# Attention block on one core: the layer-1 probabilities change partition quarters by way of memory in place of sixteen direct moves

## The chip, the cores and the metric

The kernel runs on one core of a Trainium2 chip. TensorE (PE; its weight loads are shown as PEld) multiplies, VectorE (DVE), ScalarE (ACT) and GpSimd (POOL) work on tiles in the on-chip memory SBUF, which has 128 partitions, and SyncE (SP) issues nearly all DMAs, which 16 DMA engines carry out. Each engine runs its own instructions in order, and the engines meet at semaphores. The metric is the time of one execution on the device in microseconds (us), as a median of several runs.

## What is computed

Two layers follow each other on an input of 8 batches, 512 channels and 32x32 = 1024 tokens. Layer 0 is a group norm, an attention with 8 heads, a projection and a second group norm with a residual. Layer 1, cut to what matters here, is an attention over all 512 channels:

```python
qkv = einsum('oc,bcn->bon', w_qkv, x)             # x: 8 x 512 x 1024 tokens
qkv = qkv / (sqrt(mean(square(qkv), axis=1)) + 0.0001)
q, k, v = split(qkv, 3, axis=1)
attn = softmax(einsum('bci,bcj->bij', q, k) * 512 ** -0.5, axis=-1)
h = einsum('bij,bcj->bci', attn, v)               # sums over j
out = (x + einsum('oc,bcn->bon', w_out, h)) * 2.0 ** -0.5
```

For each batch `attn` is a matrix of 1024x1024 float32 probabilities. The scores leave TensorE with the query token i on the partitions. The product with v sums over the key token j, so the probabilities have to be turned until j lies on the partitions. The change is in this turning.

## The kernel before, in words

The eight batches run one after the other: a hardware loop of seven and a last one written out, with the same body. In a batch come layer 0 (64 steps of scores, softmax, transposes and products, the longest part), its projection and second norm, and then layer 1, which is the stretch that matters here:

- **Scores.** TensorE computes eight blocks `scores1(0)` to `scores1(7)`, each of 128 query tokens by 1024 keys (48 matmuls at L514). VectorE scales a block and takes its row maxima (`scaled_max`, L1493), ScalarE takes the exponential (`exps1`, L1047), VectorE the reciprocal of the row sum (`recip1`, L1499), and GpSimd multiplies the block by it (`normalise`, L1097). Normalised block i lies in `PB[:, i, :]`, 128 partitions by 1024 columns. ScalarE writes the columns so that the four quarters of 256 columns of a block are what has to go to the four quarters of 32 partitions (`by_quarter`).
- **Exchange.** The blocks are handled in two halves, c = 0 (blocks 0 to 3) and c = 1 (blocks 4 to 7). When the last block of a half is normalised, SyncE moves the half from PB into `F`, which is the 128x4096 weight tile `W[0]`: partition quarter tq of the source, column quarter sq, goes to partition quarter sq of F. These are 16 DMAs a half (L484), each from 32 partitions to 32 partitions, 128 runs of 1 KB. Their 16 increments each go to `s_exchanged`.
- **Turning.** VectorE waits for all 16 moves and then transposes 32x32 squares out of F back into PB, one call `turn(c, s)` (L1522) for each of eight key blocks s. ScalarE copies the turned block as the high part of a split into two parts of lower precision (`turned_hi`, L1057), and VectorE subtracts it for the low part (`turned_lo`, L1528).
- **Products.** TensorE multiplies with v (`values1(c, e, s)`, L819): for a half first e = 0 and 1 together, six matmuls for each s, which waits for the low part of that s, then e = 2 and 3. A half is 96 matmuls.

The order on each engine is written out by hand. On VectorE: `scaled_max(6)`, `turn(0,0)` to `turn(0,3)` with `recip1(6)` between them, `turned_lo(0,0)` and `(0,1)`, `scaled_max(7)`, the other turns and low parts of half 0, the norm of the next batch's input, `layer_out(0)` to `(2)` (L1505), then `turn(1,0)`, `turn(1,1)`, `turned_lo(1,0)` and so on. The last normalise of half 1 comes on GpSimd after `scaled_max(7)`. On SyncE the exchange of half 0 stands behind a weight load (L475), that of half 1 behind that of half 0 and behind a wait for all eight turns of half 0 (`s_e_ready`, since F is used again), and behind both stand the stores of the output (L495) and a weight load into `W[0]` (L491) that waits for the last turn of half 1.

Of the kernel before, what the change touches and what calls it, by code (L numbers as in the profile page):

```python
# [16 lines left out]
B, C, N = 8, 512, 1024  # L17
HEADS = 8
CH = C // HEADS
P = 128  # L20
KB = C // P
# [10 lines left out]
f32 = mybir.dt.float32  # L32
# [46 lines left out]
LAG = 5  # L79
CREDIT = 1  # L80
QUARTERS = 4
EXCHANGE = QUARTERS * QUARTERS * 16


def build(nc, x, wv_t, wp_t, wqk_t, v_qkv, v_out, wo_t, vecs, consts, out):
    ctx = ExitStack()
    with ctx:
        def sb(name, shape, dt=f32):
            return ctx.enter_context(nc.sbuf_tensor(name, shape, dt))
# [4 lines left out]
        def sem(name):  # L94
            return ctx.enter_context(nc.semaphore(name))
# [6 lines left out]
        d_m = nc.dram_tensor("d_m", [P, 4096], f32)  # L102
        d_u = nc.dram_tensor("d_u", [P, 4096], f32)
        d_r = nc.dram_tensor("d_r", [N], f32)

        X = sb("X", [P, KB, N])
        XA = sb("XA", [P, KB, N])
# [4 lines left out]
        PB = sb("PB", [P, 8, N])  # L112
# [45 lines left out]
        F = W[0][:, :].bitcast(f32).rearrange("p (q t n) -> p q t n", q=QUARTERS, t=KB)  # L158

        def turned(c, s):  # L160

            return PB[:, 4 * c + s // 2, HALF * (s % 2):HALF * (s % 2) + HALF]
# [28 lines left out]
        def w_qk(pair):  # L191

            w = W[1 if pair < 2 else 0][:, 2048 * (pair % 2):2048 * (pair % 2) + 2048]
            return w.rearrange("p (h k n) -> p h k n", h=2, k=KB)
# [55 lines left out]
        s_p_norm = sem("p_norm")  # L250
# [23 lines left out]
        s_prod_sum = sem("prod_sum")  # L274
        s_sum_full = sem("sum_full")
        s_g_full = sem("g_full")
        s_exchanged = sem("exchanged")
        s_e_ready = sem("e_ready")
        s_slot_read = sem("slot_read")
# [67 lines left out]
        def big_count(b, key):  # L347

            return BIG_BASE + b * NBIG + big_at(b, key) + 1
# [5 lines left out]
        def own_wait(eng):  # L355

            eng.sem_inc(s_waited, 1)

        def src_x(b):
            return x[b].rearrange("(k p) n -> p k n", p=P)  # L360
# [3 lines left out]
        def _(sp):  # L364
# [39 lines left out]
            def stack_head(b, pair, head):  # L404

                rows = slice(64 * head, 64 * head + 64)
                s_stack = (s_stack_a, s_stack_b)[head]
                sp.wait_ge(s_nat_ready, b * 16 + 4 * pair + 4)
                own_wait(sp)
                if pair:  # L410
                    sp.wait_ge(s_big_full, big_count(b, ("s", 16 * (pair - 1) + 8 * head + 7)))
                    own_wait(sp)
                elif head:
                    sp.wait_ge(s_stack_a, (b * PAIRS + 1) * 96)
                    own_wait(sp)
                moves = [("q", 64 * head, 0, 0), ("q", 64 - 64 * head, 0, 1)]
                moves += [("kh", q, 1, 0) for q in (0, 64)] + [("kl", q, 1, 1) for q in (0, 64)]
                for kind, to, what, part in moves[::1 if pair or head else 2]:
                    sp.dma_start(stack(kind, head)[to:to + 64, :].bitcast(f32),  # L419
                                 unstacked(what, part)[rows, :].bitcast(f32))\  # L420
                      .then_inc(s_stack, 16)

            def body(b, last):

                sp.wait_ge(s_o_full, b * 24 + CREDIT)
                own_wait(sp)
                sp.wait_ge(s_stored_g, 16)
                sp.wait_ge(s_stored_m, 16)
                stack_head(b, 0, 0)
                sp.wait_ge(s_stored_qk, 48)  # L430
                own_wait(sp)
                sp.dma_start(w_qk(1).rearrange("p h k n -> p (h k n)").bitcast(f32), d_qk[1]).then_inc(ld_qk[1], 16)
                stack_head(b, 0, 1)

                sp.wait_ge(s_out_done, (b * 8 + CREDIT) * 16)
                own_wait(sp)
                sp.dma_start(X[:], src_x(b)).then_inc(s_x_res, 16)
                sp.wait_ge(s_v_full, b * 4 + 4)
                own_wait(sp)
                for i in (2, 3):  # L440
                    sp.dma_start(w_qk(i).rearrange("p h k n -> p (h k n)").bitcast(f32), d_qk[i]).then_inc(ld_qk[i], 16)
                stack_head(b, 1, 0)
                sp.dma_start(W[1][:].bitcast(f32), d_wp[:]).then_inc(s_ld_wp, 16)
                stack_head(b, 1, 1)
                stack_head(b, 2, 0)
                stack_head(b, 2, 1)
                stack_head(b, 3, 0)
                sp.wait_ge(s_stored_wv, 16)
                own_wait(sp)
                sp.dma_start(W[0][:].bitcast(f32), d_g[:]).then_inc(s_ld_g, 16)  # L450
                stack_head(b, 3, 1)
                sp.wait_ge(s_big_full, big_count(b, ("proj", KB - 1)))
                own_wait(sp)
                sp.dma_start(W[1][:].bitcast(f32), d_m[:]).then_inc(s_ld_m, 16)
                if not last:
                    sp.wait_ge(s_xc_ready, (b + 1) * KB)
                    sp.wait_ge(s_xc_lo, (b + 1) * KB)
                    own_wait(sp)
                    sp.dma_start(XA[:], src_x(b + 1)).then_inc(s_x_next, 16)
                sp.wait_ge(s_g_full, b * 2 + 2)  # L460
                own_wait(sp)
                sp.wait_ge(s_stored_u, 16)
                own_wait(sp)
                sp.dma_start(W[0][:].bitcast(f32), d_u[:]).then_inc(s_ld_u, 16)
                sp.wait_ge(s_r_col, b + 1)
                own_wait(sp)
                sp.dma_start(d_r.ap().rearrange("(s p) -> p s", p=P), rcol, allow_slow_non_contiguous=True)\
                  .then_inc(s_r_stored, 16)
                sp.wait_ge(s_r_stored, b * 16 + 16)
                own_wait(sp)  # L470
                sp.dma_start(RB[:], d_r.ap().partition_broadcast(P)).then_inc(s_r_row, 16)
                if not last:
                    sp.wait_ge(s_big_full, big_count(b, ("y", KB - 1)))
                    own_wait(sp)
                    sp.dma_start(w_qk(0).rearrange("p h k n -> p (h k n)").bitcast(f32), d_qk[0])\  # L475
                      .then_inc(ld_qk[0], 16)
                for c in range(2):
                    sp.wait_ge(s_p_norm, b * 72 + 64 + 4 * c + 4)
                    if c:
                        sp.wait_ge(s_e_ready, b * 16 + 8)  # L480
                    own_wait(sp)
                    for tq in range(QUARTERS):
                        for sq in range(QUARTERS):
                            sp.dma_start(F[32 * sq:32 * sq + 32, tq, :, :],  # L484
                                         PB[32 * tq:32 * tq + 32, 4 * c:4 * c + 4, 256 * sq:256 * sq + 256])\
                              .then_inc(s_exchanged, 16)
                for j in range(8):
                    if j == 3 and not last:
                        sp.wait_ge(s_e_ready, b * 16 + 16)
                        own_wait(sp)  # L490
                        sp.dma_start(W[0][:].bitcast(f32), d_wv[:]).then_inc(s_ld_wv, 16)  # L491
                    sp.wait_ge(s_y_out, b * 8 + j + 1 + CREDIT)
                    own_wait(sp)
                    c, e = j // 4, j % 4
                    sp.dma_start(out[b].rearrange("(k p) n -> p k n", p=P)[:, e, HALF * c:HALF * c + HALF],  # L495
                                 X[:, e, HALF * c:HALF * c + HALF]).then_inc(s_out_done, 16)

            sp.dma_start(d_wv[:], W[0][:].bitcast(f32)).then_inc(s_stored_wv, 16)
            sp.wait_ge(s_prod_lo, SETUP_BIG)
            sp.dma_start(d_u[:], product_stage(2).bitcast(f32)).then_inc(s_stored_u, 16)  # L500
            each_batch(sp, body)
            sp.wait_ge(s_out_done, (B * 8 + CREDIT) * 16)

# [668 lines left out]
        def _(dve):  # L1172
# [130 lines left out]
            def body(b, last_batch):  # L1303
# [215 lines left out]
                def turn(c, s):  # L1519
                    if s == 0:  # L1520
                        dve.wait_ge(s_exchanged, (2 * b + c + 1) * EXCHANGE)
                    V.transpose(turned(c, s).rearrange("p (t q r) -> p t q r", t=KB, q=QUARTERS),  # L1522
# [110 lines left out]
```

## Time and profile before

| | us |
|---|---|
| median of 3 runs | 3375.08 (3374.36 to 3375.76) |
| the profiled execution | 3375.88 |
| its span, first to last instruction | 3373.7 |
| TensorE busy in the span | 3351.2 (99%) |
| VectorE busy | 2132.7 (63%) |
| ScalarE busy | 1838.7 (55%) |
| GpSimd busy | 1064.3 (32%) |

All durations below come from the one profiled execution. A row of a timeline gives the start in us from the span's start, the length in us, engine, line, operation, the tiles as written <- read, and a count where neighbours are merged; in square brackets stand the engine's idle time just before and who ended it. L numbers are lines of the kernel. A row of a table by stretches gives, for each engine, the busy time and the number of instructions, then the granted TensorE clock (1.00 is the full 2.4 GHz), the mean busy share of the 16 DMA engines and what they moved. In the names of tiles, F shows as W, of which it is a view.

### The profile page before, as it was taken

To read this page: it belongs to the slowest core of one execution; us is meant where nothing else is said; L and a number is where in the kernel's file an instruction comes from. 1 tells how busy PE (TensorE), PEld (TensorE's weight loads), DVE (VectorE), ACT (ScalarE), POOL (GpSimd) and SP (SyncE) were. 2 spreads that over 40 slices of the span, in tenths; PEclk is the share of its full clock that TensorE was granted. 3 is DMA by queue.
4 is the path that set the end of the run, shared out by engine and by line. 5 is a ranking of instruction groups with operands and counts; after the bars stand their busy time and mean duration, and the time that the engine had idled before them with its cause. 6 is when DMAs were issued, how large, how long until landed. Compare 5 with 4: busy or idle time off the path is not lost.

```text
span 3373.7 us, 51950 instructions
## 1 busy us (share of the span) xinstructions
PE 3351.2 (99%) x16816; PEld 2777.5 (82%) x16816; DVE 2132.7 (63%) x3489; ACT 1838.7 (55%) x3094; POOL 1064.3 (32%) x947
## 2 busy tenths in 40 slices
PE   8999999999999999999999999999999999999999
PEld 6888888888888888888888888888888888888887
DVE  5677357773578745786457854578555784557844
ACT  4677227862378523784337842388333882347822
POOL 1344104441045410453104531145211452124511
PEclk9999999999999999999999999999999999999999
DMA  8522244313534125331253212442224422343212
GB/s 340 149 67 59 79 131 124 93 34 94 140 99 101 62 57 151 103 86 76 53 167 91 73 75 76 144 101 63 93 61 144 98 63 94 92 139 70 63 57 75
DMA packets 109871, 332.15 MB, mean 98 GB/s; under 512 B 21760, under 2 KB 54784, under 8 KB 98816
## 3 DMA queue, kind: packets, MB, share of 16 engines
q1 hardware_dynamic: 107648, 322.15, 33.3%
q10 hardware_dynamic: 1920, 6.29, 0.9%
q8 instruction: 149, 2.44, 0.3%
q14 instruction: 154, 1.26, 0.1%
HBM read 162.68 MB, written 31.49 MB: 58 GB/s over the span
## 4 chain that ended last, share of the span: by engine, by line
PE 94%; DMA 2%; issue 1%; DVE 1%; SPq 1%; ACT 1%; POOL 0%; POOLq 0%; DVEq 0%
PE big L514 25%; PE big L648 14%; PE ops L634 14%; PE tps L619 14%; PE big L746 7%; PE big L655 5%; PE tps L819 5%; PE ops L819 5%; PE ops L598 3%; DMA ST<-ST 2%; PE tps L746 1%; SPq L419 0%; PE ops L746 0%; SPq L484 0%; PE ops L788 0%
## 5 line engine op out<-in xcount | busy, mean ns | idle before, releaser
L1097 POOL TENSOR_SCALAR PB<-PB,small 128x1024 f32<-128x1024 f32 x576 | 648.7, 1127 | 1294.8 <-DVE small L1342 1277.2
L1347 DVE TENSOR_TENSOR PT<-tps,PT 128x512 fp32r<-128x512 f32 x1024 | 652.5, 679 | 42.1 <-ACT PT L954 41.7
L1336 DVE TENSOR_REDUCE small<-big 128x1 f32<-128x1024 f32 x512 | 625.2, 1221 | 85.1 <-PE big L648 81.8
L954 ACT ACTIVATE PT<-tps 128x512 fp32r<-128x512 f32 x1024 | 564.1, 597 | 158.3 <-PE tps L619 155.4
L948 ACT ACTIVATE PB<-big,small 128x1024 f32<-128x1024 f32 x512 | 572.8, 1119 | 94.8 <-DVE small L1336 91.8
L634 PE MATMUL ops<-PT,VT 128*128 128x512 f32 x2048 | 599.1, 414 | 0.0
L648 PE MATMUL big<-ST 128*128 128x512 f32 x2048 | 554.2, 392 | 3.5 <-DMA ST<-ST 3.5
L619 PEld LDWEIGHTS tps<-ident,PB 128*128 128x128 f32 x4096 | 470.2, 140 | 95.4 <-DVE PT L1347 30.9
L619 PE MATMUL tps<-ident,PB 128*128 128x128 f32 x4096 | 545.7, 274 | 0.9
L648 PEld LDWEIGHTS big<-ST 128*128 128x128 f32 x2048 | 382.6, 188 | 91.5 <-issue 6.1
L634 PEld LDWEIGHTS ops<-PT,VT 128*128 128x128 f32 x2048 | 346.1, 189 | 47.1 <-DVE PT L1347 5.0
L514 PE MATMUL big<-HH,W 128*128 128x512 f32 x1024 | 333.9, 391 | 0.8 <-issue 0.7
L1328 DVE SCALAR_TENSOR_TENSOR ST<-big,vec,ST 128x512 fp32r<-128x512 f32 x128 | 96.1, 751 | 318.8 <-ACT ST L940 318.8
L940 ACT ACTIVATE ST<-big,vec 128x512 fp32r<-128x512 f32 x128 | 88.2, 689 | 293.4 <-PE big L514 293.4
L514 PEld LDWEIGHTS big<-HH,W 128*128 128x128 f32 x1024 | 192.3, 188 | 44.7 <-issue 3.7
L1107 POOL TENSOR_TENSOR XA<-RB 64x512 f32<-64x512 f32 x128 | 163.9, 1280 | 146.9 <-ACT RB L965 145.7
L1047 ACT ACTIVATE PB<-PB,small 128x1024 f32<-128x1024 f32 x56 | 69.8, 1246 | 252.1 <-POOL small L1160 252.1
L514 PE MATMUL big<-HL,W 128*128 128x512 f32 x512 | 199.9, 390 | 0.0
L1160 POOL TENSOR_SCALAR small<-small 128x1 f32<-128x1 f32 x64 | 19.0, 297 | 518.8 <-DVE small L1493 505.4
L514 PE MATMUL big<-HH,ST 128*128 128x512 f32 x512 | 178.5, 389 | 0.0
L655 PE MATMUL big<-HH,W 128*128 128x512 f32 x512 | 168.6, 393 | 0.0
L1493 DVE CUSTOM_DVE_ANT_0 PB<-big,RB 128x1024 f32<-128x1024 f32 x56 | 68.6, 1225 | 151.4 <-PE big L514 151.4
(188 smaller groups left out, 4911.7 us busy)
## 6 DMA issues: line engine op xcount, KB each, us to landing
ST<-ST SPq DMA_DIRECT2D x360, 256.0 KB, 5.3
W<-d_qk SPq DMA_DIRECT2D x32, 1024.0 KB, 7.0
W<-PB SPq DMA_DIRECT2D x256, 128.0 KB, 2.4
X<-in_x SPq DMA_DIRECT2D x8, 2048.0 KB, 10.2
W<-d_wp SPq DMA_DIRECT2D x8, 2048.0 KB, 11.9
W<-d_g SPq DMA_DIRECT2D x8, 2048.0 KB, 11.8
W<-d_m SPq DMA_DIRECT2D x8, 2048.0 KB, 7.7
W<-d_u SPq DMA_DIRECT2D x8, 2048.0 KB, 13.2
```

The source lines that it names most:

```text
L514: last = mm(dst, stat(sp_, k), mov(mp_, k), start=(i == 0), stop=(i == n - 1))
L619: last = nc.tensor.transpose(tps[n % 2][:, P * t:P * t + P], PB[:, 4 * (u % 2) + t, P * s:P * s + P], ident[:])
L634: last = mm(ops[u % 2][:], VT[:, s, P * (u // 2):P * (u // 2) + P], pt_slot(u, s)[:, part, :], start=(s == 0 and part == 0), stop=(s == 7 ...
L648: last = mm(t[:, cols], stack("q", head)[:, tok:tok + P], stack(kind, head)[:, cols], start=(i == 0), stop=(i == 1))
L655: last = mm(t[:, cols], w_full[1][:, wp, k, P * o:P * o + P], (HH, HL)[ap][:, k, cols], start=(k == 0 and i == 0), stop=(k == PAIRS - 1 an ...
L746: last = mm(to, w_full[slot][:, wp, j, P * k:P * k + P], x1(xp, j)[:, cols], start=(j == 0 and i == 0), stop=(j == (k if slot == 0 else KB ...
L819: last = mm(out_bank(use)[:], VT[:, s, col:col + P], ptb[:, pp, :], start=(s == 0 and i == 0), stop=(s == 7 and i == 2))
L948: act_fn(PB[:, i, :], t[:], ACT.Exp, bias=negmax[:, i:i + 1], accum_out=rowsum[:, i:i + 1])\
L954: act_fn(pt_slot(u, s)[:, 0, :], tps[n % 2][:], ACT.Copy).then_inc(s_pt_hi, 1)
L1097: nc.gpsimd.tensor_scalar(PB[:, i, :], PB[:, i, :], rinv[:, i:i + 1], 1.0, ALU.mult, ALU.mult)\
L1336: V.tensor_reduce(negmax[:, i:i + 1], tile(("s", 4 * u + tb))[:], axis=AX.X, op=ALU.max, negate=True).then_inc(s_row_max, 1)
L1347: V.tensor_tensor(pt_slot(u, s)[:, 1, :], tps[n % 2][:], pt_slot(u, s)[:, 0, :].bitcast(f32), ALU.subtract).then_inc(s_pt_ready, 1)
```

## The change

Each half now goes through a buffer `d_f[c]` in the memory off the core. As soon as a block is normalised, SyncE stores it whole, 128 partitions by 4 KB, 512 KB in one DMA; the buffer's layout puts partition p of quarter q at `[p, q, t, :]`. After the fourth store SyncE waits for all four to have landed (`s_sent`), for half 1 also for the turns of half 0 as before, and then loads F with four DMAs, one for each partition quarter: 32 partitions, each of 16 runs of 1 KB, 512 KB in one DMA. VectorE now waits for the four loads. The transposes and all that comes after are the same. The diff, whole:

```diff
-EXCHANGE = QUARTERS * QUARTERS * 16
+EXCHANGE = QUARTERS * 16
...
+        d_f = [nc.dram_tensor(f"d_f{c}", [P // QUARTERS, QUARTERS, KB, N], f32) for c in range(2)]
...
+        s_sent = sem("sent")
...
                 for c in range(2):
-                    sp.wait_ge(s_p_norm, b * 72 + 64 + 4 * c + 4)
+                    for t in range(KB):
+                        sp.wait_ge(s_p_norm, b * 72 + 64 + 4 * c + t + 1)
+                        own_wait(sp)
+                        sp.dma_start(d_f[c].ap().rearrange("p q t n -> q p t n")[:, :, t, :], PB[:, 4 * c + t, :])\
+                          .then_inc(s_sent, 16)
+                    sp.wait_ge(s_sent, (2 * b + c + 1) * 16 * KB)
                     if c:
                         sp.wait_ge(s_e_ready, b * 16 + 8)
                     own_wait(sp)
-                    for tq in range(QUARTERS):
-                        for sq in range(QUARTERS):
-                            sp.dma_start(F[32 * sq:32 * sq + 32, tq, :, :],
-                                         PB[32 * tq:32 * tq + 32, 4 * c:4 * c + 4, 256 * sq:256 * sq + 256])\
-                              .then_inc(s_exchanged, 16)
+                    for q in range(QUARTERS):
+                        sp.dma_start(F[32 * q:32 * q + 32, :, :, :], d_f[c][:, :, :, 256 * q:256 * q + 256])\
+                          .then_inc(s_exchanged, 16)
```

## Rows read from the trace of the kernel before

**Rows 1.** The page: span, busy time of TensorE, granted clock in 40 slices.

```profile
span 3373.7 us, 51950 instructions
PE 3351.2 (99%) x16816; PEld 2777.5 (82%) x16816; DVE 2132.7 (63%) x3489; ACT 1838.7 (55%) x3094; POOL 1064.3 (32%) x947
PEclk9999999999999999999999999999999999999999
```

**Rows 2.** Waits over the whole span: who for whom, us in total, times, longest.

```profile
DVE PB L1522 <- DMA W<-PB: 15.9, 9, 2.4
PEld ops L819 <- DVE ST L1528: 3.7, 8, 0.5
PEld ops L819 <- DVE PT L1528: 1.7, 5, 0.4
```

**Rows 3.** Timeline of SyncE's queue in the sixth batch, both exchanges and behind.

```profile
2483.85 34.90 SPq L484 DMA_DIRECT2D W<-PB  x32
2519.01 1.72 SPq L495 DMA_DIRECT2D out<-X  x3
```

**Rows 4.** Timeline of GpSimd, sixth batch: normalise of blocks 3, 4 and 7.

```profile
2482.63 1.13 POOL L1097 TENSOR_SCALAR PB<-PB,small 128x1024 f32<-128x1024 f32 x1 [0.66 <-DVE small L1499]
...
2491.65 1.13 POOL L1097 TENSOR_SCALAR PB<-PB,small 128x1024 f32<-128x1024 f32 x1
...
2506.51 1.13 POOL L1097 TENSOR_SCALAR PB<-PB,small 128x1024 f32<-128x1024 f32 x1 [0.81 <-DVE small L1499]
```

**Rows 5.** Timeline of VectorE, sixth batch: first turns, first low parts, scaled_max(7).

```profile
2496.82 1.90 DVE L1522 STREAM_TRANSPOSE PB<-W 128x512 f32<-128x512 f32 x3
...
2499.52 1.27 DVE L1528 TENSOR_TENSOR PT<-PB,PT 128x512 fp32r<-128x512 f32 x2
2501.62 1.23 DVE L1493 CUSTOM_DVE_ANT_0 RB<-big,RB 128x1024 f32<-128x1024 f32 x1 [0.83 <-PE big L514]
...
2520.58 1.30 DVE L1522 STREAM_TRANSPOSE PB<-W 128x512 f32<-128x512 f32 x2 [1.75 <-DMA W<-PB]
2522.07 0.69 DVE L1528 TENSOR_TENSOR PT<-PB,PT 128x512 fp32r<-128x512 f32 x1 [0.19 <-ACT PT L1057]
```

**Rows 6.** Timeline of TensorE's weight loads, sixth batch: where the products begin.

```profile
2501.01 5.40 PEld L819 LDWEIGHTS ops<-PT,VT 128*128 128x128 f32 x24
...
2508.23 1.23 PEld L819 LDWEIGHTS ops<-ST,VT 128*128 128x128 f32 x6 [0.46 <-DVE ST L1528]
...
2523.10 5.40 PEld L819 LDWEIGHTS ops<-PT,VT 128*128 128x128 f32 x24
```

**Rows 7.** Timelines, half 1 of batches 2 and 5: last normalise, first turn.

```profile
853.00 1.13 POOL L1097 TENSOR_SCALAR PB<-PB,small 128x1024 f32<-128x1024 f32 x1 [0.81 <-DVE small L1499]
866.44 1.30 DVE L1522 STREAM_TRANSPOSE PB<-W 128x512 f32<-128x512 f32 x2 [1.11 <-DMA W<-PB]
...
2092.85 1.13 POOL L1097 TENSOR_SCALAR PB<-PB,small 128x1024 f32<-128x1024 f32 x1 [0.81 <-DVE small L1499]
2107.63 1.30 DVE L1522 STREAM_TRANSPOSE PB<-W 128x512 f32<-128x512 f32 x2 [2.43 <-DMA W<-PB]
```

**Rows 8.** The page's DMA issues: count, KB of each, median us from issue to landing.

```profile
out<-X SPq DMA_DIRECT2D x64, 256.0 KB, 2.4
RB<-d_r SPq DMA_DIRECT2D x8, 512.0 KB, 5.1
d_u<-PT SPq DMA_DIRECT2D x1, 2048.0 KB, 9.6
W<-d_m SPq DMA_DIRECT2D x8, 2048.0 KB, 7.7
```

**Rows 9.** Three stretches: moves ST<-ST, the exchange W<-PB, the load W<-d_m.

```profile
2152.00:2154.00 2.00, 2.00 (x10) 1.50 (x8) 0.00 (x0) 0.00 (x0) 0.00 (x0) 1.00 1.00 207
...
2488.00:2490.00 2.00, 2.00 (x11) 1.71 (x10) 0.02 (x1) 0.00 (x0) 0.00 (x0) 1.00 0.87 198
...
3227.00:3229.00 2.00, 2.00 (x12) 1.68 (x11) 1.64 (x6) 0.00 (x0) 0.01 (x1) 1.00 1.03 442
```

## The prediction

> **What bounds the kernel now.** I read the page first. TensorE is busy 99% of the span at the full granted clock [rows 1], so nothing can be won but the few waits left in its stream, and whatever makes it wait longer is added to the time. The list of waits comes next: at the products of layer 1 TensorE's weight loads wait for low parts of turned blocks, 3.7 us in eight waits and 1.7 us in five [rows 2]. VectorE waits 15.9 us in nine waits for the exchange itself [rows 2]. So the exchange sits right at the edge of TensorE's work, and the question is how much later, or earlier, F may be full.
>
> The timelines of the sixth batch answer that. I measure an exchange from the end of the last normalise of its half to the first turn and call that length E. In half 0 the normalise ends at 2482.63 + 1.13 = 2483.76 [rows 4], the first of the 16 moves is issued at 2483.85 [rows 3] and the first turn starts at 2496.82 [rows 5]: 13.06 us, with no wait in front of it. The first low part is done at about 2500.15, half of the pair that starts at 2499.52 [rows 5], and TensorE takes it at 2501.01 without a wait [rows 6], so there is 0.86 us to spare. Behind that low part stands scaled_max(7), which waits 0.83 us for TensorE [rows 5], the same slack. **Half 0 may take 13.06 + 0.85 = 13.9 us** before TensorE stands, and from there every microsecond moves both TensorE and VectorE, and by scaled_max(7) also the last normalise of half 1.
>
> In half 1 the normalise ends at 2507.64 [rows 4], and the first turn starts at 2520.58 after 1.75 us of waiting for the moves [rows 5]: E = 12.9. The first low part ends at 2522.76 [rows 5] and TensorE takes it at 2523.10 [rows 6]: **half 1 may take 12.94 + 0.34 = 13.3 us.** The eight batches vary; the shortest and the longest E of half 1 are 866.44 - 854.13 = 12.3 and 2107.63 - 2093.98 = 13.65 [rows 7]. The long ones are the waits of TensorE for PT, 1.7 us in all [rows 2], about 0.2 us a batch.
>
> **The change, part by part.**
>
> Removed: 32 issues a batch on SyncE and their moves. They ran at about 198 GB/s with the DMA engines busy at 0.87 [rows 9]; a half of 2048 KB (2097 thousand bytes) takes 10.6 us at that, and the rest of E is the way from issue to landing. SyncE's own time costs nothing: only the stores of the output stand behind it [rows 3], and no engine of this batch waits for them.
>
> Stores of the first three blocks of a half: each is issued while later blocks are still computed. The fourth normalise of a half is the last thing before the exchange, so these three are landed or nearly so by then and cost nothing; block 2 of half 0 is finished only 1.8 us before block 3, and if its 512 KB were still moving this would cost up to a part of its own length.
>
> The fourth store is new on the path. Two stores in the trace bracket it: 256 KB lands after 2.4 us, 2048 KB after 9.6 us [rows 8]. On the line between them 512 KB is 3.4 us. The bounds are 2.4 us and, by the 512 KB load, 5.1 us [rows 8]. I take 3.4.
>
> The wait on s_sent and the issue of the loads: the gap between the end of the normalise and the first issue is 0.09 us today [rows 3, 4]; I take 0.1 us twice, once for the store and once for the loads. Queued behind the waiting SyncE are the loads themselves, for half 0 the stores of half 1, and for half 1 the output stores.
>
> The loads move the same 2048 KB into F. No row shows a load from memory into 32 partitions. The nearest row by size and source is W<-d_m, the same 2048 KB into all 128 partitions: 7.7 us to landing [rows 8], at 442 GB/s in its middle [rows 9], so 4.7 us of it is transfer and 3.0 us is start and end. The nearest rows by destination are the moves between parts of the partitions: ST<-ST, 64 partitions at a time with runs of 4 KB, holds the engines at a share of 1.00 and yet moves 207 GB/s, and the exchange of today, 32 at a time with runs of 1 KB, 198 GB/s [rows 9]. So long runs do not help a move that touches half of the partitions or fewer, and I take 207 GB/s for the loads, since each one writes 32 partitions and they follow each other in one queue: 10.1 us of transfer plus 3.0 is **13.1 us**. Bounds: 7.7 us if the loads run as W<-d_m does, 13.6 us at 198 GB/s.
>
> The Trainium skill, page "SBUF — State Buffer", section "Door 1: The DMA port swizzle", states that what a transfer can reach depends on how many of 16 ports its partitions touch, and that 32 or 64 partitions from 0 touch 8, for HBM to SBUF 189 GB/s at 1 MiB with about 218 GB/s as the limit. No row here shows such a load; at 218 GB/s the transfer would be 9.6 us and the sum below 3416 us.
>
> Sum: E = 0.1 + 3.4 + 0.1 + 13.1 = **16.7 us** in place of about 13. Half 0: 16.7 - 13.9 = 2.8 us of TensorE. Half 1, counted from a last normalise that is late by the same 2.8 us as TensorE is: 16.7 - 13.3 = 3.4 us, less the 0.2 us that it waits there now, 3.2. Together 6.0 us a batch. Eight batches: 48 us. The stall of 0.46 us inside half 0 [rows 6] stays, since VectorE and TensorE shift together. Nothing later gives the time back: TensorE is the engine that is behind, and the others wait for it. The profiled execution took 3375.88 us, 0.8 us above the median of the three runs and 2.2 us more than its span; 3375.9 + 48 = **3424 us**.
>
> The granted clock is at its full level in every slice [rows 1], the first included. I price the longer stands of TensorE at no loss of clock; no row shows a stand of 3 us in mid-kernel.
>
> **The rivals.**
>
> *The loads run at full width* (the other side: not slower). If what holds ST<-ST and W<-PB is their source, which is also a part of the partitions, a load from memory is free of it. Then it takes 7.7 us, E = 0.2 + 3.4 + 7.7 = 11.3, half 0 has no wait it has not now, half 1 loses its 0.2 us: 8 x 0.2 = 1.5 us won, 3374 us. For it: both slow rows have a narrow source as well as a narrow target, so they can't tell which of the two binds. Against it: each load writes 32 partitions only, and today's 16 moves go round all four target quarters and are no quicker for it. It decides from E = 14.1 on, where (14.1 - 13.9) + (14.1 - 13.3) - 0.2 is 0.8 us a batch, 0.2% in all; that is a load of 10.5 us, or 280 GB/s.
>
> The Trainium skill, page "DMA: Bandwidth & Descriptors", section "Anatomy of one DMA — SWDGE (gpsimd) path", gives about 2.0 us plus bytes/436e3 for a DMA, and its "Rules for kernel authors" advise to make few large transfers of many small. By that the loads together would take 6.8 us and a store of 512 KB 3.2 us, and the time would come out as in this rival. The trace agrees for W<-d_m, 7.7 us, and not for ST<-ST at 207 GB/s [rows 8, 9].
>
> *Between the two*: the quarters overlap in part, and the loads run at 230 to 280 GB/s. Then a load takes 10.5 to 12.1 us, E = 14.1 to 15.7, and the time is 3383 to 3408 us.
>
> *The stores of half 1 cross the loads of half 0.* Block 4 is normalised at 2492.78 [rows 4], in the middle of loads that would run from 2487 to 2500, and its 512 KB store goes to the same engines. In today's kernel nothing is moved then but the exchange. If the store takes its share ahead of the loads' tail, half 0 is 512 KB at 207 to 442 GB/s later, 1.2 to 2.5 us, 10 to 20 us in all: 3434 to 3444 us. Against it: it is issued after the loads in the same queue.
>
> *A dearer store.* At 5.1 us [rows 8] E is 18.4, and the time is 8 x (4.5 + 4.9) = 75 us more, 3451 us.
>
> **How the numbers follow.** Forecast, E between 15.7 and 17.5, 3408 to 3437 us: 0.55. Crossing stores: 0.13. Between: 0.12. Full width: 0.16. Dearer store: 0.04. The range from 3385 to 3445 leaves out the full width and the dearest store, some 0.2. Faster by over 0.2% (6.75 us, about what a measurement of this kernel can tell from no change) is hardly possible: the exchange stands for no more than 1.7 us of TensorE's waits [rows 2]; I give it 0.02. Within 0.2%: the full width and the quickest end of what lies between, 0.15. Slower: 0.83.
>
> **What would show it.** The wait of VectorE for the exchange at L1522 should grow from 15.9 us in nine waits to some 70 in sixteen, 3.6 us in half 0 and about 5.5 in half 1, and TensorE should wait at L819 for PT 5 to 6 us a batch where it waits 0.2. The issue list should show stores at 3 to 4 us and loads at 11 to 13 us, and the stretch of the loads some 210 GB/s at a share near 1. The wait of 0.46 us for ST should stay. A rate above 280 GB/s in that stretch would make the prediction wrong, and so would a first turn of half 0 that still starts within 13.9 us of the normalise.

## The result, and the profile after

| | before | after |
|---|---|---|
| median | 3375.64 us (6 runs) | 3581.72 us (6 runs) |
| ratio | | 1.061, 95% interval 1.0596 to 1.0623 |
| span of the profiled execution | 3373.7 us | 3579.6 us |

The changed kernel is 206 us slower, 25.8 us a batch. The direction was forecast, the size was not: the forecast was 48 us more, and its range ended at 3445 us.

The page of the changed kernel, as in [rows 1]: span, busy times, and the granted TensorE clock in 40 slices.

```profile
span 3579.6 us, 51942 instructions
PE 3386.7 (95%) x16816; PEld 2801.5 (78%) x16816; DVE 2133.0 (60%) x3489; ACT 1841.6 (51%) x3094; POOL 1066.5 (30%) x947
PEclk9999999999999999999999998999989999899998
```

TensorE runs the same 16816 matmuls, and yet it is busy 3386.7 us in place of 3351.2, 35.5 us more, and the clock is no longer full in every slice. The list of waits, as in [rows 2], has the rest:

```profile
DVE PB L1527 <- DMA W<-d_f: 199.3, 16, 13.4
PE ops L824 <- DVE PT L1533: 170.6, 16, 12.1
```

And the waits of SyncE's queue:

```profile
SPq L359 <- DMA d_f<-PB: 199.0, 16, 12.8
```

TensorE now stands 170.6 us before the first product of the 16 halves. With the 35.5 us of slower matmuls that is 206.1 us, the whole difference of the spans (205.9). And SyncE waits 199.0 us, 12.4 us in the mean of the halves, for the stores to land, which the forecast had put at 3.4 us.

The timelines of the sixth batch, as in [rows 3 to 6]: SyncE's stores and loads (the second row is the fourth store of half 0 alone, from a narrower window), then the normalise of block 3 on GpSimd, the first turn on VectorE and the first products on TensorE.

```profile
2600.38 13.19 SPq L483 DMA_DIRECT2D d_f<-PB  x4
...
2613.06 0.51 SPq L483 DMA_DIRECT2D d_f<-PB  x1
2626.51 2.62 SPq L490 DMA_DIRECT2D W<-d_f  x4
2629.32 19.33 SPq L483 DMA_DIRECT2D d_f<-PB  x4
2660.96 2.59 SPq L490 DMA_DIRECT2D W<-d_f  x4
...
2611.83 1.13 POOL L1102 TENSOR_SCALAR PB<-PB,small 128x1024 f32<-128x1024 f32 x1 [0.67 <-DVE small L1504]
...
2638.31 1.90 DVE L1527 STREAM_TRANSPOSE PB<-W 128x512 f32<-128x512 f32 x3 [12.21 <-DMA W<-d_f]
...
2641.56 7.42 PE L824 MATMUL ops<-PT,VT 128*128 128x512 f32 x24 [10.97 <-DVE PT L1533]
```

In half 0, E is 2638.31 - 2612.96 = 25.35 us, where 16.7 was forecast. From the issue of the fourth store to the issue of the loads pass 13.45 us, from there to the first turn 11.8 us. The 24 matmuls behind the wait take 7.42 us; in the kernel before, the same row of TensorE's timeline has 5.60:

```profile
2501.24 5.60 PE L819 MATMUL ops<-PT,VT 128*128 128x512 f32 x24
```

Four stretches of the changed kernel show what the DMA engines and the clock did, with the columns of [rows 9]: the stores, then the loads, then the end of the wait.

```profile
2614.00:2618.00 4.00, 4.00 (x19) 3.30 (x19) 1.14 (x3) 1.33 (x2) 0.27 (x1) 1.00 0.26 97
...
2632.00:2634.00 2.00, 0.00 (x0) 0.00 (x0) 0.00 (x0) 0.00 (x0) 0.00 (x0) 1.00 1.13 223
2634.00:2636.00 2.00, 0.00 (x0) 0.00 (x0) 0.00 (x0) 0.00 (x0) 0.00 (x0) 0.74 1.13 216
2636.00:2640.00 4.00, 0.00 (x0) 0.00 (x0) 1.69 (x3) 0.94 (x2) 0.00 (x0) 0.50 0.53 134
```

The share in the stores is a quarter, 0.26, at 97 GB/s: as if four of the sixteen engines carried them. The loads ran close to the 207 GB/s that were forecast, at 216 to 223 GB/s with all engines busy. And the granted clock falls to 0.50, the level of 1.2 GHz, while TensorE stands.

A second row of the page speaks for four engines, that of the DMA packets, here of the kernel before and then of the changed one:

```profile
DMA packets 109871, 332.15 MB, mean 98 GB/s; under 512 B 21760, under 2 KB 54784, under 8 KB 98816
```

```profile
DMA packets 115247, 365.69 MB, mean 102 GB/s; under 512 B 18944, under 2 KB 51968, under 8 KB 104192
```

If each DMA leaves one small packet for each engine that it runs on, and moves and loads run on all sixteen, the 256 direct moves left 4096 of the 21760 and the 64 loads leave 1024. Then 18944 - (21760 - 4096) - 1024 = 256 are left for the 64 stores: four each.

The theory from here on: **a DMA runs on as many engines as its outermost dimension allows, and the store, whose target is ordered by quarter, partition, column, has 4 outermost.** Rivals: going through memory is dear in itself; the layout of the buffer, with 64 KB from one partition's row to the next, is what slows the stores; the fourth store is only late because it stands behind the third.

### The profile page after: what moved, and what is told of

It is laid out like the page before. It is cut to its first block, busy times and chain, and to the rows that moved or that the text cites. A ratio compares the mean times of both kernels' runs of the same rounds, so it can differ in the third digit from the quotient of the medians.

```text
span 3579.6 us, 51942 instructions
## 1 busy us (share of the span) xinstructions
PE 3386.7 (95%) x16816; PEld 2801.5 (78%) x16816; DVE 2133.0 (60%) x3489; ACT 1841.6 (51%) x3094; POOL 1066.5 (30%) x947
## 2 busy tenths in 40 slices
DMA packets 115247, 365.69 MB, mean 102 GB/s; under 512 B 18944, under 2 KB 51968, under 8 KB 104192
## 4 chain that ended last, share of the span: by engine, by line
PE 80%; DMA 12%; issue 2%; DVE 2%; ACT 1%; SPq 1%; POOL 1%; POOLq 0%; DVEq 0%; ACTq 0%
PE big L519 20%; PE big L653 13%; PE ops L639 13%; PE tps L624 13%; PE big L751 6%; DMA d_f<-PB 6%; PE big L660 5%; DMA W<-d_f 5%; PE ops L824 3%; PE ops L603 2%; PE tps L824 2%; DMA ST<-ST 2%; PE tps L751 1%; SPq L490 1%; ACT PB L1052 1%
## 5 line engine op out<-in xcount | busy, mean ns | idle before, releaser
L639 PE MATMUL ops<-PT,VT 128*128 128x512 f32 x2048 | 599.2, 414 | 0.0
L639 PEld LDWEIGHTS ops<-PT,VT 128*128 128x128 f32 x2048 | 346.1, 189 | 47.3 <-DVE PT L1352 5.0
L519 PE MATMUL big<-HH,W 128*128 128x512 f32 x1024 | 333.9, 391 | 0.4
L824 PE MATMUL ops<-PT,VT 128*128 128x512 f32 x384 | 124.3, 495 | 170.6 <-DVE PT L1533 170.6
L824 PEld LDWEIGHTS ops<-PT,VT 128*128 128x128 f32 x384 | 94.7, 252 | 200.2 <-DVE PT L1533 154.9
L1527 DVE STREAM_TRANSPOSE PB<-W 128x512 f32<-128x512 f32 x128 | 86.1, 693 | 199.3 <-DMA W<-d_f 199.3
## 6 DMA issues: line engine op xcount, KB each, us to landing
W<-d_wp SPq DMA_DIRECT2D x8, 2048.0 KB, 12.3
```

The source lines that it names most:

```text
L519: last = mm(dst, stat(sp_, k), mov(mp_, k), start=(i == 0), stop=(i == n - 1))
L639: last = mm(ops[u % 2][:], VT[:, s, P * (u // 2):P * (u // 2) + P], pt_slot(u, s)[:, part, :], start=(s == 0 and part == 0), stop=(s == 7 ...
L824: last = mm(out_bank(use)[:], VT[:, s, col:col + P], ptb[:, pp, :], start=(s == 0 and i == 0), stop=(s == 7 and i == 2))
```

## Experiments

The edits are shown against the changed kernel, or against the run that is named, without their waits, semaphore increments and counts, and with `nc.dram_tensor` and `.ap()` shortened.

**One store with 128 rows outermost.** The buffer is ordered by partition; to keep the access patterns of the loads short, they become sixteen of 128 KB.

```diff
-d_f = [dram([P // QUARTERS, QUARTERS, KB, N]) for c in range(2)]
+d_f = [dram([P, KB, N]) for c in range(2)]
...
-sp.dma_start(d_f[c].rearrange("p q t n -> q p t n")[:, :, t, :], PB[:, 4 * c + t, :])
+sp.dma_start(d_f[c][:, t, :], PB[:, 4 * c + t, :])
...
-for q in range(QUARTERS):
-    sp.dma_start(F[32 * q:32 * q + 32, :, :, :], d_f[c][:, :, :, 256 * q:256 * q + 256])
+for tq in range(QUARTERS):
+    for q in range(QUARTERS):
+        sp.dma_start(F[32 * q:32 * q + 32, tq, :, :], d_f[c][32 * tq:32 * tq + 32, :, 256 * q:256 * q + 256])
```

> The buffer is laid out by partition, so that one store of a block has 128 rows outermost in memory as well as in PB; the loads become sixteen of 128 KB as the direct moves were. In the changed kernel a half took 25.4 us from its last normalise to the first turn, 13.4 of it until the fourth store had landed, and the DMA engines stood at a share of 0.25 all through the stores. Theory A, the stores run on 4 of the 16 engines because the buffer's outermost dimension is 4: now a store lands after some 3.4 us, the share in the stores is well above 0.25, the length is about 16 us, TensorE waits some 5 us a batch and the time is 3400 to 3420 us. Theory B, writing to memory and reading it back is dear in itself: the fourth store still takes over 10 us and the time stays above 3540 us.

Measured: 3413.73 us, ratio 1.0115 (1.0098 to 1.0132). Its DMA issues (columns of [rows 8]), then SyncE's wait for the stores, then the page's packets:

```profile
d_f<-PB SPq DMA_DIRECT2D x64, 512.0 KB, 2.6
W<-d_f SPq DMA_DIRECT2D x256, 128.0 KB, 3.0
```

```profile
SPq L359 <- DMA d_f<-PB: 38.1, 16, 2.8
```

```profile
DMA packets 119087, 365.71 MB, mean 107 GB/s; under 512 B 22784, under 2 KB 55808, under 8 KB 108032
```

The same 512 KB now land in 2.6 us. The wait for the stores falls from 199.0 to 38.1 us, and 168 of the 206 us are gone. The small packets are 17664 + 320 x 16 = 22784, sixteen for each of the 64 stores and 256 loads. E is 15.3 to 16.7 us in the halves of this run, where 16.7 was forecast. That memory is dear in itself falls.

**The buffer as it was, each store cut into four.**

```diff
-sp.dma_start(d_f[c].rearrange("p q t n -> q p t n")[:, :, t, :], PB[:, 4 * c + t, :])
+for q in range(QUARTERS):
+    sp.dma_start(d_f[c][:, q, t, :], PB[32 * q:32 * q + 32, 4 * c + t, :])
```

> The buffer's layout and the four loads stay as in the changed kernel; only the store of a block is cut into four, one for each partition quarter, so that 32 is outermost in each. Theory A (too few engines): the fourth block's stores land after 4 to 5 us, the length is about 16 to 17 us, the time 3405 to 3425 us. Theory C, the layout of the buffer (rows of one partition 64 KB apart) is what slows the stores: the stores stay at some 100 GB/s, the length stays at 25 us and the time above 3540 us, while the run with the other layout is quick.

Measured: 3434.71 us, ratio 1.0175 (1.0158 to 1.0192), 10 us above the expected range. Its DMA issues, and from the timeline of TensorE the first products of both halves in the sixth batch:

```profile
d_f<-PB SPq DMA_DIRECT2D x256, 128.0 KB, 2.3
W<-d_f SPq DMA_DIRECT2D x64, 512.0 KB, 7.9
```

```profile
2541.09 5.73 PE L824 MATMUL ops<-PT,VT 128*128 128x512 f32 x24 [1.17 <-DVE PT L1533]
...
2567.08 7.37 PE L824 MATMUL ops<-PT,VT 128*128 128x512 f32 x24 [3.68 <-DVE PT L1533]
```

With 32 outermost the stores into the same layout are quick, so the layout falls. E is 15.5 to 17.9 us. The 10 us above the range fit the clock: after a wait of 1.17 us the 24 matmuls take 5.73 us, after one of 3.68 us they take 7.37. The forecast's sum with this run's mean E, 16.0 and 17.1 us in the two halves, gives 46 of the 59 us by which its span is longer, and 13 us are left.

**Two outermost in place of four.** This asks the theory for a second size of the effect.

```diff
-sp.dma_start(d_f[c].rearrange("p q t n -> q p t n")[:, :, t, :], PB[:, 4 * c + t, :])
+for h in range(2):
+    sp.dma_start(d_f[c].rearrange("p q t n -> q p t n")[2 * h:2 * h + 2, :, t, :], PB[64 * h:64 * h + 64, 4 * c + t, :])
```

> The changed kernel with each store of a block cut into two of 256 KB, each with 2 outermost in memory where the whole store has 4. Theory, the outermost dimension sets how many of the 16 engines a store runs on: now two, a share of 0.13 and some 50 GB/s in the stores, which fall behind the blocks; a half takes over 40 us in the first half and over 30 in the second, and the time is 3700 us or more, although the stores are more in number. Rival, it is the size of one DMA or its runs of 4 KB: two stores at a time are no slower than one, and the time is at most 3580 us.

Measured: 3853.66 us, ratio 1.1416 (1.1394 to 1.1437). A stretch of its stores and one of its loads, then its packets:

```profile
2790.00:2794.00 4.00, 4.00 (x21) 3.40 (x20) 1.04 (x5) 0.89 (x2) 0.62 (x1) 1.00 0.13 53
...
2814.00:2818.00 4.00, 0.00 (x0) 0.00 (x0) 0.00 (x0) 0.00 (x0) 0.00 (x0) 0.50 1.03 219
```

```profile
DMA packets 115247, 365.69 MB, mean 95 GB/s; under 512 B 18944, under 2 KB 51968, under 8 KB 104192
```

Half the share, 0.13, and half the rate, 53 GB/s, although twice as many stores are under way: with four engines as with two, each carries some 24 to 27 GB/s. The 18944 small packets are those of the changed kernel, now for 128 stores in place of 64, so two each. At any time two engines carry the stores; whether both stores of a block share the same two, or one follows the other, no row shows, since none names the engines. E is 43 to 44 us in half 0 and about 42 in half 1, and both, like the time, are in what was expected (over 40, over 30, 3700 us or more).

The Trainium skill, page "DMA: Bandwidth & Descriptors", section "Why a DMA increments its semaphore by 16 and not by 1", states this rule: a DMA is split over the largest number of engines up to 16 that divides the slowest dimension of both sides, and a DMA that SyncE issues takes the lowest-numbered ones. The runs here agree with the number: 128 and 32 outermost run wide, 4 at a share of 0.26, 2 at 0.13. Which engines they are no run here shows.

**The fourth store without a third in front of it.** Only the stores of the first three blocks are cut.

```diff
+if t < KB - 1:
+    for q in range(QUARTERS):
+        sp.dma_start(d_f[c][:, q, t, :], PB[32 * q:32 * q + 32, 4 * c + t, :])
+else:
     sp.dma_start(d_f[c].rearrange("p q t n -> q p t n")[:, :, t, :], PB[:, 4 * c + t, :])
```

> The changed kernel, with the stores of the first three blocks of a half cut into quarters as in the run with quarter stores, and the fourth store left as it is, one DMA with 4 outermost. It parts the fourth store's own time from its wait behind the third. Theory: alone it moves 512 KB at 100 GB/s, 5.2 us, and lands after about 7 us; a half takes 19 us from the last normalise to the first turn, TensorE waits some 11 us a batch, and the time is 3455 to 3480 us with what the clock costs. Rival, the 13.4 us are all the fourth store's own: the half stays at 25 us and the time above 3560 us.

Measured: 3532.75 us, ratio 1.0467 (1.0447 to 1.0486), between the two. SyncE's timeline in the sixth batch, half 0, and two stretches of that store:

```profile
2583.84 0.61 SPq L487 DMA_DIRECT2D d_f<-PB  x1
2593.97 2.61 SPq L494 DMA_DIRECT2D W<-d_f  x4
```

```profile
2587.00:2590.00 3.00, 3.00 (x16) 2.50 (x15) 0.27 (x2) 0.53 (x2) 0.00 (x0) 1.00 0.24 51
2590.00:2593.00 3.00, 3.00 (x15) 2.47 (x14) 1.13 (x2) 1.33 (x2) 1.36 (x2) 1.00 0.18 75
```

Alone the fourth store still takes 10.1 us. By this run 10.1 of the 13.45 us of the changed kernel are its own, and 3.3 are the wait behind the third. The expected 7 us supposed the 97 to 103 GB/s of the busy queue; alone the four engines move 51 GB/s at a share of 0.24 first, and then 75 GB/s at a share of only 0.18. So they are slow in the store's first part and not in its last; why is not settled.

**What the clock costs.** TensorE is kept busy while it waits, with matmuls whose result the product overwrites.

```diff
 for c in range(2):
+    if c:
+        pe.wait_ge(s_y_out, b * 8 + 1 + CREDIT)
+    for i in range(48):
+        mm(ops[0][:], VT[:, 0, 0:P], x1(0, 0)[:, 0:HALF], start=True, stop=True)
     for s in range(NT):
         values1(c, 0, s)
```

> The changed kernel with 48 matmuls more of 512 columns before the first product of each half, into a bank that the product starts anew; they take 10.9 us of the 11 us in which TensorE waits. Theory of the clock: the granted clock stays at 1.00, the first 24 matmuls of each half take some 5.6 us where they took 7.4, and the time falls by 16 x 1.8 = 29 us to about 3553 us. Rival: these matmuls are slow because the low parts come one by one; then the time stays at 3582 us within 5.

Measured: 3565.23 us, 16.5 us less than the changed kernel, against 29 expected. The loads of the sixth batch's half 0 with the clock beside them, and the first products:

```profile
2617.00:2621.00 4.00, 4.00 (x20) 3.30 (x19) 0.00 (x0) 0.00 (x0) 0.00 (x0) 1.00 1.11 211
2621.00:2625.00 4.00, 4.00 (x19) 3.34 (x18) 0.00 (x0) 0.00 (x0) 0.00 (x0) 1.00 1.13 212
```

```profile
2631.02 5.74 PE L825 MATMUL ops<-PT,VT 128*128 128x512 f32 x24 [1.97 <-DVE PT L1538]
```

The clock stays at 1.00, but for one short stretch in the seventh batch, and the 24 matmuls take 5.74 us. So the slow matmuls are the clock's. Not all of the 35.5 us comes back, for two reasons. In three batches of this run E of half 0 is 27.2 to 27.3 us where the others have 25.4 to 26.0; why is open. And most of the rest was never lost. In the changed kernel the 96 products of half 0 take 14.4 us more than before, in all batches, and those of half 1 17.2. What half 0 loses is hidden: the last normalise of half 1 waits for VectorE and not for these products, so TensorE stands that much less at half 1, 79.0 us where the forecast's sum with the measured E has 93.6.

**The loads: narrow target or source in memory?** The stores do the permuting, to a buffer of [4, 32, 4, KB, 256], the layout of F, and F is loaded with one DMA of 128 partitions.

```diff
+to = d_f[c].rearrange("q p s t r -> p q s t r")
 for t in range(KB):
+    for tq in range(QUARTERS):
+        sp.dma_start(to[:, :, tq, t, :], PB[32 * tq:32 * tq + 32, 4 * c + t, :].rearrange("p (q r) -> p q r", q=QUARTERS))
...
+sp.dma_start(F.rearrange("p q t n -> p (q t n)"), d_f[c].rearrange("q p s t r -> (q p) (s t r)"))
```

> The stores do the permuting: each block goes out in four DMAs of 32 partitions, in runs of 1 KB, to a buffer that has the layout of F, and F is loaded whole with one DMA of 128 partitions after all four blocks have landed. Theory, a load into 32 partitions is held to some 210 GB/s by its narrow target: now the load takes about 7.7 us as the load of the weights does, the half 12 to 13 us, TensorE's waits are those of the kernel before and the time is 3372 to 3380 us. Rival, it is the source in memory that holds the loads: the load stays at 11 to 12 us, the half at 16 us and the time at 3410 us or more.

Measured: 3380.51 us, ratio 1.0017 (1.0008 to 1.0027). Its DMA issues and a stretch of the load:

```profile
W<-d_f SPq DMA_DIRECT2D x16, 2048.0 KB, 8.5
```

```profile
2494.00:2495.00 1.00, 1.00 (x6) 0.81 (x6) 0.07 (x2) 0.43 (x1) 0.73 (x2) 1.00 1.01 426
```

The same 2048 KB from memory now move at 426 GB/s, twice the rate of the loads into 32 partitions at the same share of the engines, and land after 8.5 us. The source in memory is not what held them. (The runs on the side of F are longer here, 16 KB, so width and length change together; the next run parts them.) E is 12.2 to 14.9 us in half 1, up to two microseconds over the 12 to 13 that were expected. TensorE's weight loads wait 5.2 us for PT where they waited 1.7 [rows 2], and that is most of the small loss:

```profile
PEld ops L826 <- DVE PT L1535: 5.2, 7, 1.7
```

**Can the way through memory win?** Blocks 0 to 2 are loaded while block 3 is being stored. Against the run with the wide load (`last_f` is `d_f[c]` with F's 128 partitions outermost):

```diff
-sp.dma_start(F.rearrange("p q t n -> p (q t n)"), d_f[c].rearrange("q p s t r -> (q p) (s t r)"))
+sp.dma_start(F[:, :, 0:KB - 1, :].rearrange("p q t n -> p q (t n)"), last_f[:, :, 0:KB - 1, :].rearrange("p s t r -> p s (t r)"))
+sp.wait_ge(s_sent_last, (2 * b + c + 1) * 16 * QUARTERS)
+sp.dma_start(F[:, :, KB - 1, :], last_f[:, :, KB - 1, :])
```

> As the run with the wide load, but blocks 0 to 2 are loaded as soon as the stores of block 3 are issued, and block 3 alone (512 KB in runs of 1 KB, 128 partitions) after its own stores have landed. The half should take 9 to 10 us. Theory, the exchange stood for no more than 1.7 us of TensorE's waits before: the time is 3371 to 3375 us, no difference that can be measured from the kernel before. Rival, other waits hang on the exchange too: over 5 us faster than before.

Measured: 3375.78 us, ratio 1.000 (0.9991 to 1.001). TensorE's waits at the products, as in [rows 2]:

```profile
PEld ops L831 <- DVE ST L1540: 3.8, 8, 0.5
PEld ops L831 <- DVE PT L1540: 0.9, 3, 0.3
```

The whole loss is gone and no more: the waits for PT fall from 1.7 to 0.9 us, too little to be seen. E of half 1 is 12.0 to 13.6 us and not 9 to 10, since the last load, 512 KB, waits behind the 1536 KB in front of it and lands after 6.9 to 8.3 us.

This last load goes into all 128 partitions in runs of 1 KB, the length of the narrow loads' runs. In half 0 of the sixth batch there is a stretch in which 162 of the 169 data packets that the DMA engines start are its 1 KB runs:

```profile
2491.50:2492.00 0.50, 0.50 (x4) 0.42 (x3) 0.00 (x0) 0.50 (x1) 0.50 (x1) 1.00 1.04 375
```

They move at 375 GB/s, against 216 to 223 GB/s for runs of 1 KB into 32 partitions. So it is the width of the target that holds the narrow loads, and not the length of the runs.

Three further runs tried to use the time that half 0 gains, by the order on VectorE and ScalarE. (The eight turned blocks of a half lie in the tiles PT, ST and W, four, two and two.)

Turns ahead, on top of the run with the loads ahead:

```diff
+turn(0, 0)
+turn(0, 1)
+turn(0, 2)
 scaled_max(6)
-turn(0, 0)
-turn(0, 1)
-turn(0, 2)
-recip1(6)
 turn(0, 3)
+recip1(6)
```

> As the run with the loads ahead, and VectorE does the first three turns of half 0 before scaled_max(6), in the 2 us in which it waits there. Theory: the low parts come earlier, the wait of 0.46 us inside half 0 goes too, and the time falls by 8 x 0.6 = 5 us to 3368 to 3372 us. Rival, scaled_max(6) is held back by turns that still wait for the loads: TensorE waits for its buffer at the scores and the time is 3376 us or more.

Low parts ahead, on top of it:

```diff
+turn(0, 4)
+turned_lo(0, 2)
+turn(0, 5)
 scaled_max(7)
-turned_lo(0, 2)
-turn(0, 4)
 turned_lo(0, 3)
-turn(0, 5)
 turned_lo(0, 4)
```

> As the run with the turns ahead, where TensorE still waited 0.46 us in each batch for a low part on ST; here turn(0,4), turned_lo(0,2) and turn(0,5) stand before scaled_max(7) on VectorE, in time that it had free. Theory: these waits, 3.7 us in all, hang on the two turns and the low part that came after scaled_max(7); they go, and the time falls to 3370 to 3374 us. Rival: the low parts on ST wait for the copies of ScalarE, which come after the last exponential; then the waits and the time (3376 to 3377 us) stay.

Copies ahead, on top of both; on VectorE turned_lo(0, 5) also moves ahead of recip1(7), and on ScalarE:

```diff
-for s in range(4):
+for s in range(6):
     turned_hi(0, s)
 exps1(7)
-for s in range(4, NT):
+for s in range(6, NT):
     turned_hi(0, s)
```

> As the run with the low parts ahead, and ScalarE copies turned blocks 4 and 5 of half 0 before the last exponential, in the 3.5 us in which it waits there for scaled_max(7); VectorE takes the low part of block 5 before recip1(7). If the low parts on ST wait for ScalarE's copies and for nothing else, TensorE has no wait for ST any more (3.7 us in the kernel before, over 17 us in the run with the low parts ahead), and the time is 3369 to 3373 us, under the kernel before. Rival: the last exponential is held back by the two copies and the second half comes later; then the time is 3377 us or more.

Measured, in this order: 3376.79 us, ratio 1.0003 (0.9994 to 1.0012); 3388.97 us, ratio 1.0038 (1.0024 to 1.0053); 3391.67 us, ratio 1.0048 (1.0034 to 1.0062). TensorE's longest waits for low parts in the three, one row of the first, one of the second and two of the third, and for the second run the low part of block 4 on VectorE:

```profile
PEld ops L831 <- DVE ST L1540: 3.7, 8, 0.5
```

```profile
PEld ops L831 <- DVE ST L1540: 17.1, 16, 1.5
```

```profile
PEld ops L831 <- DVE PT L1540: 13.6, 9, 3.2
PEld ops L831 <- DVE W L1540: 5.6, 8, 0.9
```

```profile
2515.47 0.70 DVE L1540 TENSOR_TENSOR ST<-PB,ST 128x512 fp32r<-128x512 f32 x1 [2.06 <-ACT ST L1069]
```

The wait of 0.46 us a batch for ST does not hang on the exchange. In the second run the low part of block 4 waits for ScalarE's copy behind the last exponential, as its rival had it; but that exponential comes later too, since scaled_max(7) now stands behind what was put ahead of it, and the 12 us by which the time rose are in neither the theory nor the rival. In the third the waits for ST are gone, and others for PT and W stand in their place: what is put ahead of scaled_max(7) holds back the last exponential, and with it half 1. All three expectations of a gain fell, and none of these versions beats the kernel before.

## Why the prediction was wrong

- **The bound and the slack: right.** The whole loss lies in TensorE's stream, before the first products of the halves. The forecast's own sum with the measured E of the changed kernel, 25.75 us in half 0 and 25.2 in half 1 in the mean of eight batches, gives 8 x (11.85 + 11.9 - 0.2) = 188 us; with the 16.5 us that the run with TensorE kept busy gave back it is 205 of the 206 us. Of the 158 us that the forecast missed, the stores make 154 and the clock some 18, and the loads, quicker than forecast, take 14 back.
- **The fourth store: wrong, and the step that failed.** "On the line between them 512 KB is 3.4 us": it took 13.4 us in the mean of half 0 and 12.9 in that of half 1, the wait behind the third store included. The line went through out<-X and d_u<-PT [rows 8], both with 128 rows outermost on both sides, and so shown only for DMAs that use all engines. This store lies between the two in bytes, but has 4 outermost. With 128 outermost it lands after 2.6 us, better than forecast. The bound of 5.1 us, from a load of 512 KB, said nothing of such a store either.
- **The first three stores: wrong by 3.3 us.** They were costed at nothing because they are issued early. On four engines they keep the queue busy up to the fourth, which waits behind the third.
- **The loads: right in kind, 0.9 us too high.** 13.1 us were forecast, 11.8 to 12.9 passed from their issue to the first turn, 12.25 in the mean of the sixteen halves; 207 GB/s was taken, 216 to 223 was measured. With that the rival that the forecast gave 0.16, loads at full width, fell, and the runs with the wide load and with the loads ahead show why: into all 128 partitions memory gives 426 GB/s, and 375 GB/s in runs of 1 KB.
- **The clock: wrong.** It was priced at nothing with the remark that no row shows a stand of 3 us in mid-kernel. Stands of 9 to 12 us bring it to 0.50, matmuls take 35.5 us more in all, and 16.5 us came back when TensorE was kept busy. At waits like those that were forecast it costs some 4 to 13 us in all: that is what the forecast's sum with the measured E leaves over in the runs with 128 rows outermost (waits up to 3.0 us) and with quarter stores (up to 4.3 us).
- **The crossing stores of half 1: not seen.** The loads of half 0 moved 216 to 223 GB/s in the stretches shown, with the store of block 4 issued behind them at 2629.32, and they took 12.3 us in the mean, less than was forecast without a crossing.
- **The kernel that the forecast described in fact** is the one with 128 rows outermost. It took 3413.7 us, inside the range of the forecast case, 3408 to 3437, but in part by luck, since two terms are off in opposite ways: its E, 15.7 us in the mean, is the case's lower end, and the clock, priced at nothing, adds some 4 us.

Of what was named as a sign that the forecast holds, the stretch of the loads came, 216 to 223 GB/s at a share above 1. The waits came in kind and not in size: 199.3 us at L1527 where 70 were named, and 21 us a batch for PT where 5 to 6 were. Three signs failed. "Stores at 3 to 4 us" is the one that matters. The issue list of the changed kernel has its loads at 7.9 us and not at 11 to 13, since it counts each of the four by itself. And the wait for ST did not stay: behind the slow products of PT the list of waits has none.

## What to carry to other kernels

Before a DMA is costed from a row with the same number of bytes, compare the outermost dimension of both sides: a view that permutes can put a small one outermost, and the transfer then runs on no more engines than that, four and two here. A share of the DMA engines that stands still at 0.25 or 0.13 while one queue is all that moves is the sign of it. A round trip through memory costs its store's landing and its load's start in series, so let the stores permute, load wide, and load what is already there while the last block is being stored.

## What was not expected of the hardware

- The same 512 KB of runs of 4 KB land after 2.6 us with 128 outermost and after 10.1 us, alone, with 4, on a quarter of the engines; two queued stores with 4 outermost move 97 to 103 GB/s, one alone 51 GB/s in its first part and 75 in its last 3 us.
- Loads from memory into 32 partitions move 211 to 223 GB/s with all engines busy, into 128 partitions 426 GB/s, and 375 GB/s in runs of the same 1 KB.
- After TensorE has stood 11 us the granted clock is 0.50 and 24 matmuls take 7.42 us; with TensorE kept busy through the same wait it is 1.00 and they take 5.74 us.
